# Three gaps of padding between the tiles of a gated cross-attention and expert kernel

## The chip, the cores and the metric

The kernel runs on one core of a Trainium2 chip. The time is that of one execution on the device, in microseconds. The median of three runs before the change is 463.22 us (463.19 to 463.77).

## What is computed

The input x is 16 batches of 128 tokens of 128 numbers. First comes a gated cross-attention: x is normalised, queries come from it, keys and values from a context of 77 rows of 96 numbers for each batch, with 16 heads of 8 numbers; the result goes through an output projection and is added to x with a gate. Then comes a gated mixture of experts over all 2048 tokens, in four rounds:

```
for r in range(4):
    logits = flat @ Wg[r] + bg[r]                 # four experts
    w = softmax(top 2 of logits)
    hmid = gelu(flat @ W1[e] + b1[e])             # 128 -> 512, every expert
    y = hmid @ W2[e] + b2[e]                      # 512 -> 128
    cur = cur + sum over e of w[e] * y[e]
```

All four experts are computed for every token, and each is weighed by its share, which is zero for two of them.

## The kernel before

All of it stands in SBUF, 128 partitions, in float32. The attention part runs batch by batch and ends at about 88 us; the transposes of the probabilities (L1275) use a stretch of the tile `below` as weights and the tile `ident` as moving operand, the sums over the values (L1297) use `v_st`, the sums of the probabilities (L1303) use `row_head`. The expert part is a loop over 64 units: four rounds, in each four chunks of 512 tokens, for each chunk four experts. Its order on every engine is written out by hand, and semaphores join the engines.

For precision each product is made of three matmuls. An operand is split in a high part, rounded to the format that TensorE takes (fp32r), and a low part, the remainder. A unit's first layer, `up(u)`, has four column blocks k; for each it issues high x high (L1395), low tokens x high weights (L1396) and high tokens x low weights (L1397), all 128x128 weights and 512 moving columns, into PSUM bank k. ACT takes the bank through the gelu into `g_sb` (L806) and makes `h_hi` (L813); DVE makes `h_lo` (L948). The second layer, `down(u)`, does the same three passes (L1408, L1409, L1410) over four blocks, all twelve into one PSUM bank, 4 or 5 by turns. DVE weighs the result (L958) and adds it to `cur` (L969). TensorE runs `up(u + 1)` before `down(u)`, so that the gelu of one unit stands beside matmuls of its neighbours. The last unit's second layer is done in two halves of 256 columns (L1423 to L1425).

Tiles are placed one after the other in the order in which the program declares them, each on a multiple of 32 bytes of a partition. In the program before, those of the two layers start at these bytes:

```
w1_hi  23648   w1_lo  31840      first-layer weights; block (e, k) is 2048 e + 512 k further
w2_hi  40032   w2_lo  48224      second-layer weights; the same steps
x_sb   56416   xn     65248   v_st 75104   probT 95584
cur   105824   x_lo  114016   x_hi 122208   tokens; chunk c is 2048 c further
cwb_even 132992   cwb_odd 149376   contrib 165760   g_sb 169856
h_hi  178048   h_lo  194432      activations; block k is 2048 k further, odd units 8192
```

`below`, `kT`, `q_st`, `k_st`, `xnT` and `ctxT` of the attention part share the bytes behind `cwb_even` with the tiles of the last two lines; `below` starts at 186272, and its second half (from block 5 on) is 2464 further in a partition.

Of the kernel before, what the change touches and what calls it, by code (L numbers as in the profile page):

```python
# [5 lines left out]
P = 128  # L6
# [9 lines left out]
def flamingo_gated_block(  # L16
# [59 lines left out]
    with ExitStack() as stack:  # L76
        def sb(name, shape, dt=F32):
            return stack.enter_context(nc.sbuf_tensor(name, shape, dt))
# [33 lines left out]
        lgs = sb("lgs", [P, 2, P])  # L112
        w1_hi = sb("w1_hi", [P, E * F], F32R)
        w1_lo = sb("w1_lo", [P, E * F], F32R)
        w2_hi = sb("w2_hi", [P, E * NF * D], F32R)
        w2_lo = sb("w2_lo", [P, E * NF * D], F32R)

# [12 lines left out]
        v_sb = sb("v_sb", [M, NC, NZ, HQ * DH, TC * PAIRS])  # L130
        probT = sb("probT", [P, 2, PAIRS * BLOCKS, L])

        cur = sb("cur", [P, N])
        x_lo = sb("x_lo", [P, NC, CH], F32R)
        x_hi = sb("x_hi", [P, NC, CH], F32R)
# [9 lines left out]
        wgt = sb("wgt", [P, TP, E])  # L145
        cw = sb("cw", [P, 2, E, TC])
        cwT = sb("cwT", [TP * E, P])
        cwb_even = sb("cwb_even", [P, 2, E, CH])

        attention = ExitStack()  # L150
# [1413 lines left out]
```

## Time and profile before

| | |
|---|---|
| median of the runs | 463.22 us |
| profiled execution, device time | 463.65 us |
| its span, first to last instruction | 461.9 us |
| TensorE busy | 452.0 us, 98% |
| DVE busy | 364.3 us, 79% |
| ACT busy | 359.9 us, 78% |
| GpSimd busy | 70.0 us, 15% |
| granted TensorE clock | 1.000 |

Matmuls are pipelined: one is counted as busy from its first read to its last result, while the next has already begun. Busy times of matmuls therefore add up to more than the time they take, and the pace is read from the distance between their starts.

### The profile page before, as it was taken

What the parts mean: (1) busy time and instruction counts of PE and PEld (TensorE: products, weight loads), DVE (VectorE), ACT (ScalarE), POOL (GpSimd) and SP (SyncE); (2) the same over time, 40 slices, a digit from 0 to 9 for tenths busy, and PEclk for the clock granted to TensorE, in tenths of its full rate; (3) what the DMA queues carried; (4) which work ended last, traced back from release to release, by engine and by line L of the source; (5) the groups of instructions that cost most, each with busy time, mean ns of one, the idle gap of its engine ahead of it and who ended that gap; (6) DMA issues with size and microseconds to landing.
All of it is one profiled execution on the core that took longest, in us unless ns stands there. A gap on an engine that the chain in (4) does not pass through costs nothing.

```text
span 461.9 us, 8784 instructions
## 1 busy us (share of the span) xinstructions
PE 452.0 (98%) x2856; PEld 355.4 (77%) x2856; DVE 364.3 (79%) x729; ACT 359.9 (78%) x742; POOL 70.0 (15%) x109
## 2 busy tenths in 40 slices
PE   8999999899999999999999999999999999999996
PEld 6666677678787888788878887888788878888885
DVE  6988989888878688768876887688768876887776
ACT  4777877696969779877987798778877887787873
POOL 6939884313000000000000000000000000000000
PEclk9999999999999999999999999999999999999999
DMA  6690000140020101300220022003100310023001
GB/s 163 191 202 17 1 9 11 32 154 3 0 92 24 70 2 43 143 0 1 67 118 1 1 87 99 0 2 113 72 0 0 141 45 1 0 80 128 24 0 45
DMA packets 12892, 25.18 MB, mean 55 GB/s; under 512 B 4615, under 2 KB 8496, under 8 KB 10800
## 3 DMA queue, kind: packets, MB, share of 16 engines
q1 hardware_dynamic: 9408, 22.23, 14.1%
q0 software_dynamic: 2784, 2.18, 2.6%
q8 instruction: 23, 0.38, 0.3%
q10 hardware_dynamic: 656, 0.23, 0.2%
q14 instruction: 21, 0.17, 0.1%
HBM read 22.82 MB, written 1.18 MB: 52 GB/s over the span
## 4 chain that ended last, share of the span: by engine, by line
PE 89%; DVE 6%; issue 2%; ACT 1%; DMA 1%; SPq 0%; POOL 0%; DVEq 0%; POOLq 0%
PE ps L1408 13%; PE ps L1410 13%; PE ps L1409 13%; PE ps L1395 12%; PE ps L1397 12%; PE ps L1396 12%; PE ps L1275 3%; PE ps L1297 2%; PE ps L1261 2%; PE ps L1303 2%; DVE least L897 1%; DVE rT_sb L913 1%; DMA x_sb<-in_x_dram 1%; PE ps L1310 1%; PE ps L1362 1%
## 5 line engine op out<-in xcount | busy, mean ns | idle before, releaser
L948 DVE TENSOR_TENSOR h_lo<-g_sb,h_hi 128x512 fp32r<-128x512 f32 x256 | 170.1, 688 | 76.0 <-ACT h_hi L813 76.0
L806 ACT ACTIVATE g_sb<-ps,cols 128x512 f32<-128x512 f32 x256 | 174.1, 691 | 41.4 <-PE ps L1397 40.8
L813 ACT ACTIVATE h_hi<-g_sb 128x512 fp32r<-128x512 f32 x256 | 155.5, 638 | 0.0
L1408 PE MATMUL ps<-h_hi,w_hi 128*128 128x512 f32 x252 | 102.4, 406 | 0.1
L1395 PE MATMUL ps<-x_hi,w_hi 128*128 128x512 f32 x256 | 101.0, 395 | 0.0
L1397 PE MATMUL ps<-x_hi,w_lo 128*128 128x512 f32 x256 | 100.1, 391 | 0.0
L1396 PE MATMUL ps<-x_lo,w_hi 128*128 128x512 f32 x256 | 99.8, 390 | 0.0
L1410 PE MATMUL ps<-h_hi,w_lo 128*128 128x512 f32 x252 | 99.6, 395 | 0.0
L1409 PE MATMUL ps<-h_lo,w_hi 128*128 128x512 f32 x252 | 99.4, 394 | 0.0
L1408 PEld LDWEIGHTS ps<-h_hi,w_hi 128*128 128x128 f32 x252 | 47.3, 188 | 14.0 <-issue 2.7
L1397 PEld LDWEIGHTS ps<-x_hi,w_lo 128*128 128x128 f32 x256 | 48.0, 188 | 11.4
L1396 PEld LDWEIGHTS ps<-x_lo,w_hi 128*128 128x128 f32 x256 | 48.1, 188 | 10.8
L1395 PEld LDWEIGHTS ps<-x_hi,w_hi 128*128 128x128 f32 x256 | 48.0, 188 | 10.8
L1410 PEld LDWEIGHTS ps<-h_hi,w_lo 128*128 128x128 f32 x252 | 47.2, 187 | 11.7
L1409 PEld LDWEIGHTS ps<-h_lo,w_hi 128*128 128x128 f32 x252 | 47.3, 188 | 9.9
L969 DVE TENSOR_TENSOR cur<-cur,contrib 128x512 f32<-128x512 f32 x63 | 43.2, 685 | 0.0
L723 ACT ACTIVATE probT<-ps 128x512 f32<-128x512 f32 (+1 forms) x48 | 25.0, 553 | 11.7 <-PE ps L1275 11.3
L713 ACT ACTIVATE below<-ps,least 128x77 f32<-128x77 f32 x128 | 29.3, 343 | 5.4 <-DVE least L897 5.3
L897 DVE TENSOR_REDUCE least<-ps 128x8 f32<-128x616 f32 x32 | 25.0, 790 | 0.4 <-PE ps L1261 0.4
L958 DVE SCALAR_TENSOR_TENSOR contrib<-ps,cols,cwb_even 128x512 f32<-128x512 f32 x32 | 23.9, 747 | 0.9 <-PE ps L1410 0.6
L1275 PE MATMUL ps<-ident,below 128*128 128x128 f32 (+1 forms) x160 | 24.0, 280 | 0.6 <-ACT probT L723 0.5
L739 ACT ACTIVATE th<-half_d 128x32 f32<-128x32 f32 (+1 forms) x10 | 2.3, 225 | 27.6 <-DVE half_d L1026 27.6
(126 smaller groups left out, 394.9 us busy)
## 6 DMA issues: line engine op xcount, KB each, us to landing
cwb_even<-cw_rows SPq DMA_DIRECT2D x8, 1024.0 KB, 5.5
cwb_odd<-cw_rows SPq DMA_DIRECT2D x8, 1024.0 KB, 4.9
w_hi<-in_L_ffn_W_dram POOLq DMA_DIRECT2D x2, 1024.0 KB, 10.4
w_in<-in_L_ffn_W_dram SPq DMA_DIRECT2D x1, 1024.0 KB, 5.6
x_sb<-in_x_dram SPq DMA_DIRECT2D x3, 256.0 KB, 5.1
out_dram<-xn SPq DMA_DIRECT2D x3, 256.0 KB, 2.5
ctxT<-in_ctx_dram SPq DMA_DIRECT2D x3, 115.5 KB, 4.7
v_st<-v_sb SPq DMA_DIRECT2D x14, 19.2 KB
```

Source lines behind the costliest of these rows:

```text
L806: nc.scalar.activation(g_sb[:, k, :], ps[:, k, :], ACT.Gelu_apprx_tanh, bias=b1_c[:, e * NF + k:e * NF + k + 1]).then_inc(gelu_done, 1)
L813: nc.scalar.activation(h_hi[:, u % 2, k, :], g_sb[:, k, :], ACT.Copy).then_inc(hi_done, 1)
L897: nc.vector.tensor_reduce(least[:, b % 2, :].rearrange("p (q h) -> p q h", q=NQ)[:, two, :], scores, AX.X, ALU.min).then_inc(least_done[ha ...
L948: nc.vector.tensor_tensor(h_lo[:, u % 2, k, :], g_sb[:, k, :], h_hi[:, u % 2, k, :].bitcast(F32), ALU.subtract).then_inc(lo_done, 1)
L969: nc.vector.tensor_tensor(cc, cc, contrib[:, u % 2, :], ALU.add).then_inc(added, 1)
L1275: t = tr(bank(key)[0:n, o:o + L], below[:, b % 2, at:at + n], ident[:, :])
L1395: mm(ps[:, k, :], w1_hi[:, w], x_hi[:, c, :], start=True, stop=False)
L1396: mm(ps[:, k, :], w1_hi[:, w], x_lo[:, c, :], start=False, stop=False)
L1397: mm(ps[:, k, :], w1_lo[:, w], x_hi[:, c, :], start=False, stop=True).then_inc(w1_done, 1)
L1408: mm(yb, w2_hi[:, w], hh, start=k == 0, stop=False)
L1409: mm(yb, w2_hi[:, w], hl, start=False, stop=False)
L1410: m = mm(yb, w2_lo[:, w], hh, start=False, stop=k == NF - 1)
```

## The change

Three tiles are declared that nothing reads or writes. The first, 32 bytes a partition, stands between the weights of the first and of the second layer. The second, 480 bytes, stands ahead of `cur`. The third, 768 bytes, stands ahead of `cwb_even`. Everything behind each is pushed along: the second-layer weights and the attention tiles behind them by 32 bytes, the tokens and the router's tiles by 512, `cwb_even` and all that follows by 1280. Instructions, their order and their semaphores stay.

```
         w1_lo = sb("w1_lo", [P, E * F], F32R)
+        pad_second = sb("pad_second", [P, 8])
         w2_hi = sb("w2_hi", [P, E * NF * D], F32R)
...
         probT = sb("probT", [P, 2, PAIRS * BLOCKS, L])
 
+        pad_tokens = sb("pad_tokens", [P, 120])
         cur = sb("cur", [P, N])
...
         cwT = sb("cwT", [TP * E, P])
+        pad_routes = sb("pad_routes", [P, 192])
         cwb_even = sb("cwb_even", [P, 2, E, CH])
```

## Rows read from the trace of the kernel before

**Rows 1.** Busy time of the engines, share of the span, instructions.
```profile
PE 452.0 (98%) x2856; PEld 355.4 (77%) x2856; DVE 364.3 (79%) x729; ACT 359.9 (78%) x742; POOL 70.0 (15%) x109
```

**Rows 2.** The chain that ended last, by engine and by line.
```profile
PE 89%; DVE 6%; issue 2%; ACT 1%; DMA 1%; SPq 0%; POOL 0%; DVEq 0%; POOLq 0%
PE ps L1408 13%; PE ps L1410 13%; PE ps L1409 13%; PE ps L1395 12%; PE ps L1397 12%; PE ps L1396 12%; PE ps L1275 3%; PE ps L1297 2%; PE ps L1261 2%; PE ps L1303 2%; DVE least L897 1%; DVE rT_sb L913 1%; DMA x_sb<-in_x_dram 1%; PE ps L1310 1%; PE ps L1362 1%
```

**Rows 3.** Windows of eight units: length, busy per engine, PEclk, DMA, GB/s.
```profile
220.00:264.00 44.00, 44.00 (x198) 35.03 (x197) 33.60 (x62) 35.27 (x65) 0.00 (x0) 1.00 0.13 49
```

**Rows 4.** Groups: shapes, count, busy us, mean ns, idle before, releaser.
```profile
L806 ACT ACTIVATE g_sb<-ps,cols 128x512 f32<-128x512 f32 x256 | 174.1, 691 | 41.4 <-PE ps L1397 40.8 <-DVE h_lo L948 0.4
L948 DVE TENSOR_TENSOR h_lo<-g_sb,h_hi 128x512 fp32r<-128x512 f32 x256 | 170.1, 688 | 76.0 <-ACT h_hi L813 76.0
L813 ACT ACTIVATE h_hi<-g_sb 128x512 fp32r<-128x512 f32 x256 | 155.5, 638 | 0.0
...
L1397 PE MATMUL ps<-x_hi,w_lo 128*128 128x512 f32 x256 | 100.1, 391 | 0.0
...
L1409 PE MATMUL ps<-h_lo,w_hi 128*128 128x512 f32 x252 | 99.4, 394 | 0.0
L1396 PEld LDWEIGHTS ps<-x_lo,w_hi 128*128 128x128 f32 x256 | 48.1, 188 | 10.8
...
L1409 PEld LDWEIGHTS ps<-h_lo,w_hi 128*128 128x128 f32 x252 | 47.3, 188 | 9.9
```

**Rows 5.** Timeline of one unit: start us, duration us, engine and line.
```profile
249.68 0.39 PE L1395 MATMUL ps<-x_hi,w_hi 128*128 128x512 f32 x1
...
251.07 0.39 PE L1395 MATMUL ps<-x_hi,w_hi 128*128 128x512 f32 x1
...
252.43 0.40 PE L1408 MATMUL ps<-h_hi,w_hi 128*128 128x512 f32 x1
252.43 0.19 PEld L1409 LDWEIGHTS ps<-h_lo,w_hi 128*128 128x128 f32 x1
...
255.23 0.40 PE L1395 MATMUL ps<-x_hi,w_hi 128*128 128x512 f32 x1
```

**Rows 6.** Timeline, head of another second layer, all engines.
```profile
257.99 0.40 PE L1408 MATMUL ps<-h_hi,w_hi 128*128 128x512 f32 x1
...
258.22 0.39 PE L1409 MATMUL ps<-h_lo,w_hi 128*128 128x512 f32 x1
...
258.45 0.40 PE L1410 MATMUL ps<-h_hi,w_lo 128*128 128x512 f32 x1
...
258.51 0.23 ACT L739 ACTIVATE th<-half_d 128x32 f32<-128x32 f32 x1 [3.32 <-DVE half_d L1026]
```

**Rows 7.** Timeline of TensorE, the loop's first first layer.
```profile
88.62 0.40 PE L1396 MATMUL ps<-x_lo,w_hi 128*128 128x512 f32 x1
...
90.00 0.39 PE L1396 MATMUL ps<-x_lo,w_hi 128*128 128x512 f32 x1
...
90.91 0.39 PE L1397 MATMUL ps<-x_hi,w_lo 128*128 128x512 f32 x1
```

**Rows 8.** Timeline of TensorE, last unit, first and twelfth half matmul.
```profile
454.43 0.28 PE L1423 MATMUL ps<-h_hi,w_hi 128*128 128x256 f32 x1
...
455.72 0.28 PE L1425 MATMUL ps<-h_hi,w_lo 128*128 128x256 f32 x1
```

**Rows 9.** Timeline of TensorE, two groups of four transposes of one batch.
```profile
79.81 0.60 PE L1275 MATMUL ps<-ident,below 128*104 128x128 f32 x4
...
80.60 0.60 PE L1275 MATMUL ps<-ident,below 128*128 128x128 f32 x4
```

**Rows 10.** Groups of weight loads of 32 columns.
```profile
L1303 PEld LDWEIGHTS ps<-probT,row_head 128*32 128x32 f32 x320 | 10.9, 110 | 0.3 <-issue 0.3
L1297 PEld LDWEIGHTS ps<-probT,v_st 128*32 128x32 f32 x320 | 10.6, 142 | 6.2 <-issue 6.2
```

More of the change, by code:

```diff
@@ L114, in flamingo_gated_block @@
         w1_lo = sb("w1_lo", [P, E * F], F32R)
+        pad_second = sb("pad_second", [P, 8])
         w2_hi = sb("w2_hi", [P, E * NF * D], F32R)
@@ L131, in flamingo_gated_block @@
         probT = sb("probT", [P, 2, PAIRS * BLOCKS, L])
+        pad_tokens = sb("pad_tokens", [P, 120])
         cur = sb("cur", [P, N])
@@ L147, in flamingo_gated_block @@
         cwT = sb("cwT", [TP * E, P])
+        pad_routes = sb("pad_routes", [P, 192])
         cwb_even = sb("cwb_even", [P, 2, E, CH])
```

## The prediction

> **What bounds the kernel now.** I read the busy shares first, then the chain of waits, then the windows, then the timeline of TensorE. The reader is to see in this order: TensorE is busy in 98% of the span, DVE and ACT in 79 and 78% [rows 1]; the chain that ended last is 89% TensorE, and its six largest lines are the six matmuls of the experts, 13% or 12% each [rows 2]; from 220 us to 264 us, eight units of the expert loop, TensorE has no idle time at all while ACT is busy for 35.27 us of 44 and DVE for 33.60 [rows 3]. So nothing that TensorE waits for matters in the expert loop; what counts is how fast one 128x512 matmul follows another. DVE and ACT wait for the others of the loop (76.0 us and 41.4 us of idle time before their two lines [rows 4]) and have room.
>
> Busy times of pipelined matmuls overlap (about 395 ns each [rows 4]), so the price of one is the distance from start to start. In one unit of the steady loop [rows 5] the second layer starts at 252.43 and the next first layer at 255.23: 12 matmuls in 2.80 us, 233.3 ns each. The first layer before it runs from 249.68 to 252.43: 12 in 2.75 us, 229.2 ns each, of which the first six take 1.39 us (231.7 each) and the last six 1.36 us (226.7 each). 512 columns at 2.4 GHz, the level that the granted clock of 1.00 in [rows 3] is, are 213.3 ns. So each matmul pays 13.4 ns over its columns at best and 20 ns in the second layer. The two layers have the same shapes, the same three passes, the same weight load (188 ns each in both [rows 4]) beside each matmul: the load of the next weights starts in the same hundredth as the matmul before it (252.43 and 252.43 in [rows 5]). What differs is which bytes are read, and which PSUM banks are written.
>
> I looked at three other explanations. Traffic of DVE and ACT: from 257.99 to 258.45, at the head of a second layer, ACT is at the end of 3.32 us of idle time and DVE does instructions of 32 columns, and the matmuls still come at 0.23 and 0.23 us, no faster than with both busy [rows 6]. Waiting: none. The break between layers: after a pause in which TensorE started no matmul of the experts, the first layer also has some slow ones, from 88.62 to 90.00 six in 1.38 us, then four in 0.91 us [rows 7]; so the slow start of the first layer is partly its own and is not all owed to the second layer. In the last unit, with 256 columns each, eleven second-layer matmuls take 1.29 us [rows 8], 117.3 ns against 106.7 ns for the columns: 10.6 ns over, about half of what the full ones pay. The surcharge grows with the length of the moving stream, as reads that disturb one another would.
>
> **The change part by part.** No instruction is added, removed or moved, no wait and no DMA changes; 1280 bytes a partition are left empty. What changes is where operands start.
>
> Second layer. w2_hi and w2_lo move from 40032 and 48224 to 40064 and 48256; h_hi and h_lo from 178048 and 194432 to 179328 and 195712. Modulo 64 bytes the weights stood at 32 and the moving operand at 0; afterwards both stand at 0. Their distance h_hi - w2_hi was 138016, which is 800 modulo 2048, and becomes 139264, which is 0 modulo 2048 (17 times 8192). In the first layer, the faster one, w1_hi at 23648 and x_hi at 122208 already agree modulo 64 (both 32) and modulo 256 (both 96); their distance is 98560, 256 modulo 2048. My reading is that the layer in which weight and moving operand disagree modulo 64 pays 6.6 ns more per matmul, and that the change takes this away. The trace does not prove it: it has one placement for each layer. If the second layer falls to the 226.7 ns of [rows 5], a unit saves 2.80 - 2.72 = 0.08 us. There are 63 full units (252 executions of each of the three lines [rows 4], four a unit), so 63 x 0.08 = 5.0 us. The bound on this side is that the first six of each first layer go to 226.7 too, 1.39 - 1.36 = 0.03 us a unit, 1.9 us more, 6.9 in all; [rows 7] speaks against it, so I leave it out of the sum. A further bound is the surcharge of the half matmuls, 10.6 ns: both layers at 223.9 ns would save 5.55 - 24 x 0.2239 = 0.18 us a unit, 11 us.
>
> First layer. w1 stays, x_lo and x_hi move by 512 to 114528 and 122720. Modulo 512 nothing changes (both at 352), modulo 1024 the distance goes from 256 to 768. The four weight blocks of a layer lie 512 bytes apart and so already run through both distances modulo 1024, and the last two blocks are equally fast in [rows 5]. I take nothing. The bounds: 1.9 us of gain (above), and on the other side the 233.3 ns of the other layer for all twelve, 12 x 0.2333 - 2.75 = 0.05 us a unit, 3.1 us of loss.
>
> What ACT, DVE and the stores read and write. cur by 512, cwb, contrib, g_sb by 1280, all by whole multiples of 256. Their instructions have steady durations (691, 638, 688 ns [rows 4]) and stand beside a full TensorE; they cost nothing as long as that covers them. If TensorE's unit shrinks to 5.47 us, ACT, with 4 x (691 + 638) ns = 5.3 us of overlapping work and 4.4 us of real busy time a unit (35.27 / 8), still fits. So no new wait is late next; TensorE stays the bound.
>
> The attention part, up to 88 us. x_sb, xn, v_st and probT move by 32, and below, kT, q_st and k_st by 1280. Here weight loads limit: four transposes take 0.60 us whether their block of `below` starts at 32 modulo 64 (all four of the group at 80.60) or at 0 (three of the four at 79.81) [rows 9]. So 32 bytes alone move nothing that is seen there. A weight load does feel how its columns lie: 32 columns of v_st, taken 32 bytes apart, take 142 ns where 32 adjacent ones of row_head take 110 [rows 10]; the step between them is not changed. I take 0, with 0.3 us to either side.
>
> Here the Trainium skill speaks against the change. Its page "TensorE: Matmul & The Clock Gate", section "Step-by-step: what each phase is for", says that TensorE has two independent SBUF read ports, one for the moving operand and one for the weights, so that loading does not take bandwidth from the running matmul. By that rule, neither layer should mind its placement and the time stays; that is the first rival below. The two layers' 229.2 and 233.3 ns don't follow from it, though they don't refute it. The page "SBUF — State Buffer", section "Specifications (TRN2)", gives cachelines of 16 bytes; all three shifts are multiples of 16, so by it too nothing would change, and no run here shows the size of such a line.
>
> Sum: the profiled execution took 463.65 us, span 461.9. 463.65 - 5.0 = 458.65. Against the median of 463.22 the same difference gives 458.2 us.
>
> **The rivals.** No change: the slower pace of the second layer belongs to something else, such as its twelve accumulations into one PSUM bank where the first layer changes banks every three. For it: the second and third passes of the first layer also stay in their bank; that speaks against. For it also: 32 bytes moved nothing in [rows 9]. Time 463.2.
>
> Slower: weight and moving operand of the second layer now start at the same byte modulo 8192, at the same moment [rows 5]. If the memory is built in parts by address, the two reads meet in one part from the first column, and the pace gets worse instead of better. That decides if disturbance comes from being in the same place, not from being out of step. Priced with another step of the size seen between the layers, 6.6 ns: 63 x 12 x 6.6 ns = 5.0 us, 468.2. The same rival in the other layer, if x at its new distance loses the 226.7 ns: 466.3. Both: 471.3.
>
> Smaller gain: only part of the second layer follows, as only half of the first does now: 2.5 us, 460.7. Larger gain: 6.9 us, 456.3, up to 452 by the bound of 11 us. With the back-to-back figure of 215.7 ns that the page "TensorE: Matmul & The Clock Gate" states, section "Wait — 56ns, not 53.3ns?", an estimate would be 24 x 63 x (231.3 - 215.7) ns = 24 us less; nothing in the trace comes near that pace beside weight loads.
>
> **How the numbers follow.** The forecast with the larger gain (452 to 459.5) has 0.46, the smaller gain 0.11, no change 0.17, slower 0.26 (second layer 0.15, first layer 0.08, both 0.03). What a measurement of this kernel can tell from no change is 0.2%, 0.9 us. So faster 0.57, same 0.17, slower 0.26. The likeliest case's own range is 455.5 to 459.5. The range for 8 in 10 reaches down to 454, which leaves out some 0.03, and up to 467.5, which takes in the loss in the first layer and leaves out most of the loss in the second, 0.16.
>
> **What would show it.** In the timeline of the changed kernel, the distance from the first L1408 to the next L1395 is 2.72 us if right, 2.80 for no change, 2.88 for the slower rival; the first layer stays at 2.75. TensorE stays without idle time from 220 to 440 us, the start of the expert loop stays at 88.3 us within 0.3, and the durations of L806, L813 and L948 stay within 5 ns (the idle time before them shrinks). The prediction is wrong in its cause if the gain sits in the first layer or before 88 us, or if DVE or ACT change their durations.

## The result, and the profile after

The changed kernel takes 460.79 us (median of 4 runs, 460.51 to 460.91) where the kernel before took 463.21 us beside it; the ratio is 0.9942, with a 95% interval from 0.9929 to 0.9954. That is 2.4 us faster. The forecast was 458.2 us, 5.0 us faster, with 455.5 to 459.5 as the range of its likeliest case and 454 to 467.5 as the range for 8 in 10.

The span of the profiled execution went from 461.9 to 459.1 us. The page of the kernel after shows where to look and where not: DVE is as busy as before [rows 1], TensorE 3.5 us less.

```profile
PE 448.5 (98%) x2856; PEld 355.1 (77%) x2856; DVE 364.3 (79%) x729; ACT 360.1 (78%) x742; POOL 70.1 (15%) x109
```

The window of the steady loop, for [rows 3], has TensorE without idle time as before, at the same clock, and two more matmuls in the same 44 us (200 for 198).

```profile
220.00:264.00 44.00, 44.00 (x200) 35.33 (x199) 33.96 (x64) 35.65 (x66) 0.00 (x0) 1.00 0.12 49
```

The groups of the kernel after, for [rows 4] (three lines further down in the program, so L951 is the old L948): durations on DVE and ACT are the same within 3 ns, the idle time ahead of them is 2.4 and 2.8 us less.

```profile
L951 DVE TENSOR_TENSOR h_lo<-g_sb,h_hi 128x512 fp32r<-128x512 f32 x256 | 170.1, 688 | 73.6 <-ACT h_hi L816 73.6
L809 ACT ACTIVATE g_sb<-ps,cols 128x512 f32<-128x512 f32 x256 | 174.7, 694 | 38.6 <-PE ps L1400 37.9
L816 ACT ACTIVATE h_hi<-g_sb 128x512 fp32r<-128x512 f32 x256 | 156.0, 641 | 0.0
```

The timeline of TensorE in the kernel after, for [rows 5] (start us, duration us):

```profile
251.26 0.39 PE L1411 MATMUL ps<-h_hi,w_hi 128*128 128x512 f32 x1
...
252.64 0.39 PE L1411 MATMUL ps<-h_hi,w_hi 128*128 128x512 f32 x1
...
254.01 0.39 PE L1398 MATMUL ps<-x_hi,w_hi 128*128 128x512 f32 x1
...
255.40 0.39 PE L1398 MATMUL ps<-x_hi,w_hi 128*128 128x512 f32 x1
...
256.76 0.39 PE L1411 MATMUL ps<-h_hi,w_hi 128*128 128x512 f32 x1
```

The second layer runs from 251.26 to 254.01: 12 matmuls in 2.75 us where it was 2.80. But it has taken on the form of the first layer: six matmuls in 1.38 us (230 ns each), then six in 1.37. The first layer from 254.01 to 256.76 is unchanged in length, 2.75 us, with its slow half still ahead of its fast one. Within it something moved. On the mean of the 35 that have second layers directly on both sides, its first matmul fell from 236.6 to 230.0 ns, and its last rose from 226.6 to 235.0.

For the sums below I took all start-to-start distances of the trace. A layer of 12 that nothing interrupts (35 second layers, 53 first layers) took 2.803 and 2.755 us before and takes 2.754 and 2.751 after. Over all 63 second layers, with those where a transpose stands ahead, the mean fell by 42 ns, 2.7 us in all; the first layers give 0.1 us and the start of the loop, 88.31 to 88.20 us, another 0.1. That is the 2.8 us of the span, within the rounding.

### The profile page after: what moved, and what is told of

It is laid out like the page before. It is cut to its first block, busy times and chain, and to the rows that moved or that the text cites. A ratio compares the mean times of both kernels' runs of the same rounds, so it can differ in the third digit from the quotient of the medians.

```text
span 459.1 us, 8784 instructions
## 1 busy us (share of the span) xinstructions
PE 448.5 (98%) x2856; PEld 355.1 (77%) x2856; DVE 364.3 (79%) x729; ACT 360.1 (78%) x742; POOL 70.1 (15%) x109
## 4 chain that ended last, share of the span: by engine, by line
PE 87%; DVE 6%; issue 3%; ACT 2%; DMA 1%; SPq 0%; POOL 0%; ACTq 0%; DVEq 0%; POOLq 0%
PE ps L1411 13%; PE ps L1413 12%; PE ps L1412 12%; PE ps L1398 12%; PE ps L1399 12%; PE ps L1400 12%; PE ps L1278 3%; PE ps L1300 2%; PE ps L1264 2%; PE ps L1306 2%; ACT g_sb L809 1%; DVE least L900 1%; DVE rT_sb L916 1%; DMA x_sb<-in_x_dram 1%; PE ps L1313 1%
## 5 line engine op out<-in xcount | busy, mean ns | idle before, releaser
L951 DVE TENSOR_TENSOR h_lo<-g_sb,h_hi 128x512 fp32r<-128x512 f32 x256 | 170.1, 688 | 73.6 <-ACT h_hi L816 73.6
L1412 PE MATMUL ps<-h_lo,w_hi 128*128 128x512 f32 x252 | 98.1, 389 | 0.0
```

Of the source, the lines that this page charges most:

```text
L951: nc.vector.tensor_tensor(h_lo[:, u % 2, k, :], g_sb[:, k, :], h_hi[:, u % 2, k, :].bitcast(F32), ALU.subtract).then_inc(lo_done, 1)
L1412: mm(yb, w2_hi[:, w], hl, start=False, stop=False)
```

## The experiments

All of them change placement alone. Two numbers describe each of them: the distance, modulo 256 bytes, from the weights' first byte to that of the moving operand in each layer (x_hi - w1_hi and h_hi - w2_hi; the low parts lie a multiple of 256 bytes away and have the same, except in e8, where both distances are given, high part first), and where the moving operands themselves stand modulo 256. Paces are the means of layers that nothing interrupts.

| kernel | distance, layers 1 / 2 | x, h at (modulo 256) | 12 matmuls, layers 1 / 2, us | time, us |
|---|---|---|---|---|
| before | 0 / 32 | 96, 128 | 2.755 / 2.803 | 463.2 |
| the change | 0 / 0 | 96, 128 | 2.751 / 2.754 | 460.8 |
| e1 | 64 / 64 | 160, 192 | 2.761 / 2.748 | 461.3 |
| e2 | 0 / 32 | 96, 128 | 2.755 / 2.803 | 463.4 |
| e3 | 32 / 0 | 128, 128 | 2.793 / 2.728 | 462.4 |
| e4 | 0 / 0 | 128, 128 | 2.721 / 2.720 | 457.6 |
| e5 | 0 / 128 | 96, 224 | 2.736 / 2.792 | 461.8 |
| e6 | 128 / 128 | 0, 0 | 2.789 / 2.789 | 464.6 |
| e7 | 96 / 192 | 0, 128 | 2.807 / 2.793 | 466.3 |
| e8 | 240 and 112 / 120 and 248 | 128, 0 | 2.798 / 2.802 | 465.8 |
| e9 | 0 / 0 | 96, 96 | 2.722 / 2.720 | 457.4 |
| e10 | 240 / 248 | 128, 128 | 2.799 / 2.768 | 464.1 |
| e11 | 224 / 160 | 128, 128 | 2.801 / 2.811 | 466.3 |

**e1, the 32 bytes without the large shifts.** The small gap ahead of the second-layer weights as in the change, and one of 32 bytes ahead of the tokens.

```
+        pad_second = sb("pad_second", [P, 8])
+        pad_tokens = sb("pad_tokens", [P, 8])
```

> Only the disagreement modulo 64 is mended: second-layer weights +32 bytes, tokens and activations +64 (x stays at 32 modulo 64 like w1, h stays at 0 modulo 64, now like w2). The distance h_hi - w2_hi is 832 modulo 2048, not 0. Theory 'phase' (weight and moving operand agree modulo 64): second layer 2.75 us per 12 matmuls instead of 2.80, time 460.4 to 461.2, the whole of the change's gain. Rival 'distance' (the gain is from the distance being 0 modulo 2048): second layer stays at 2.80 us, time 463.2.

461.28 us, ratio 0.9958 (0.9943 to 0.9973). Most of the gain is there (2.1 us of the 2.4), so 0 modulo 2048 is not what counts. But the plain rule of agreement modulo 64 isn't confirmed either: with 64 between the operands no layer settles at 226.7 ns; from the fourth on its matmuls run at 227.3 to 230.4, 228.8 on the mean, in both layers.

**e2, the large shifts without the 32 bytes.**

```
+        pad_tokens = sb("pad_tokens", [P, 128])
+        pad_routes = sb("pad_routes", [P, 192])
```

> The change without its 32 bytes: weights of both layers stay, tokens +512, activations +1280. Theory 'phase': the second layer still disagrees modulo 64, 2.80 us, first layer 2.75, time 463.0 to 463.5. Rival 'distance' (the large shifts bring it): the distance is 32 modulo 2048, nearly 0, second layer 2.75 to 2.77, time about 461.5.

463.36 us, ratio 1.0001 (0.9992 to 1.0011). The timeline shows the second layer from 251.98 to 254.78, 2.80 us, as before:

```profile
251.98 0.40 PE L1410 MATMUL ps<-h_hi,w_hi 128*128 128x512 f32 x1
254.78 0.40 PE L1397 MATMUL ps<-x_hi,w_hi 128*128 128x512 f32 x1
257.54 0.40 PE L1410 MATMUL ps<-h_hi,w_hi 128*128 128x512 f32 x1
```

The shifts of 512 and 1280 bytes do nothing by themselves; both are multiples of 256. The 32 bytes of the weights are the change.

**e3, the first layer put out of step.** The change, with the tokens 32 bytes further and the activations where the change has them.

```
+        pad_second = sb("pad_second", [P, 8])
-        pad_tokens = sb("pad_tokens", [P, 120])
+        pad_tokens = sb("pad_tokens", [P, 128])
-        pad_routes = sb("pad_routes", [P, 192])
+        pad_routes = sb("pad_routes", [P, 184])
```

> As the change, but the tokens are moved by 544 instead of 512 bytes, so x stands at 0 modulo 64 and w1 at 32; the second layer is that of the change. Theory 'phase': the first layer goes from 2.75 to 2.80 us per 12 matmuls, the second keeps 2.75 or less, so the time is back at about 463.5 to 464. Rival 'distance': 32 bytes more matter little, first layer 2.75, time 460.8.

462.41 us, ratio 0.9981 (0.9971 to 0.9990): slower than the change, but less than expected. The timeline:

```profile
249.16 0.39 PE L1398 MATMUL ps<-x_hi,w_hi 128*128 128x512 f32 x1
251.95 0.39 PE L1411 MATMUL ps<-h_hi,w_hi 128*128 128x512 f32 x1
254.68 0.39 PE L1398 MATMUL ps<-x_hi,w_hi 128*128 128x512 f32 x1
```

The first layer went from 2.75 to 2.79 us, as the theory of agreement asks: the slow pace has moved to the other layer with the 32 bytes, so it does not belong to the PSUM bank or to the layer. The second layer went to 2.73, better than in the change, though nothing of it was touched: its first matmul after the first layer already runs at 226.6 ns. What is new is that x and h stand at the same place modulo 256. And one matmul in it is slow: the last, beside which weights of the first layer are loaded, at a distance of 32 again (234.8 ns on the mean of 35 layers, its eleven neighbours 226.6 to 226.8). The first layer shows the same from the other side: its last matmul, beside which second-layer weights load at a distance of 0, takes 226.6 ns and the eleven before it 230.8 to 235.0. So it is the load beside a matmul whose distance counts.

**e4, all four operands at one place.** The gap of 32 bytes stands ahead of the first-layer weights instead of the second-layer weights.

```
+        pad_first = sb("pad_first", [P, 8])
+        pad_tokens = sb("pad_tokens", [P, 128])
+        pad_routes = sb("pad_routes", [P, 184])
```

> All four operands at 0 modulo 64: weights of both layers +32, tokens +544, activations +1280. Theory 'phase' in its plain form: both layers 2.75, time 460.8. Its stronger form (the six slow matmuls at each change of layer come from the two layers standing at different places modulo 64): both layers 12 x 226.7 ns = 2.72 us, 63 x 0.07 us less than the change, 456.5. Rival 'distance': first layer 2.75, second 2.75, 460.8.

457.64 us, ratio 0.9875 (0.9859 to 0.9892), 3.2 us better than the change. Where nothing interrupts them both layers take 2.72 us, with no slow start:

```profile
249.91 0.39 PE L1411 MATMUL ps<-h_hi,w_hi 128*128 128x512 f32 x1
252.63 0.39 PE L1398 MATMUL ps<-x_hi,w_hi 128*128 128x512 f32 x1
255.35 0.39 PE L1411 MATMUL ps<-h_hi,w_hi 128*128 128x512 f32 x1
258.07 0.39 PE L1398 MATMUL ps<-x_hi,w_hi 128*128 128x512 f32 x1
```

The time is 1.1 us above the 456.5 of the stronger form. The 28 second layers that follow a transpose or another matmul outside the experts still start slowly; e9, below, shows one.

**e5, all at 96 modulo 128.** Only the activations move, by 96 bytes; every gap named `pad_routes` stands ahead of `cwb_even`.

```
+        pad_routes = sb("pad_routes", [P, 24])
```

> Weights and tokens stay; only the activations move, by 96 bytes, so that all four operands stand at 96 modulo 128 instead of 0 as in the version with all at 0. If only the agreement counts: 226.7 ns for every matmul, 457.6 us. If the common place must be at the start of a 64- or 128-byte block: no better than the change, 460.8 us or more.

461.83 us, ratio 0.9967 (0.9952 to 0.9982). The time is in the range of the second outcome, but not for the reason written there: the second layer stayed slow, 2.792 us. At 96 modulo 128 it agrees with its weights, but modulo 256 it is 128 away, so this run doesn't tell whether the common place matters. It points to a period longer than 128, which e6 tests; e9 then puts all four at 96 modulo 256.

**e6, a distance of 128 in both layers.**

```
+        pad_first = sb("pad_first", [P, 8])
+        pad_tokens = sb("pad_tokens", [P, 160])
+        pad_routes = sb("pad_routes", [P, 184])
```

> As the version with all at 0, but tokens and activations 128 bytes further, so that moving operand and weights agree modulo 128 and disagree modulo 256. If the period is 128 bytes: 226.7 ns for every matmul, 457.6 us. If it is 256 bytes or more: slower, by the 233.3 ns of a disagreement up to 467.

464.60 us, ratio 1.0025 (1.0015 to 1.0034). It differs from e4 by 128 bytes between weights and moving operands and by nothing else, and both layers go from 2.72 to 2.79 us. The period is more than 128. In e4 the distance is 256 modulo 512 in the first layer and 0 in the second, and both are equally fast: the period that fits all runs here is 256 bytes.

**e7, distances of 96 and 192.**

```
+        pad_first = sb("pad_first", [P, 16])
+        pad_second = sb("pad_second", [P, 8])
+        pad_tokens = sb("pad_tokens", [P, 16])
+        pad_routes = sb("pad_routes", [P, 24])
```

> Both moving operands at 0 modulo 128, first-layer weights at 32 (distance 96 modulo 128), second-layer weights at 64 (distance 64). From the runs before: distance 64 gave about 228.8 ns, distance 32 gave 233.3, 0 gave 226.7. Expected: second layer 12 x 228.8 = 2.75 us; first layer, if a distance of 96 is like one of 32, 2.80 us; time about 463.5. If distance 96 behaved like 0 instead, the first layer would be 2.72 us and the time 459.

466.28 us, ratio 1.0058 (1.0043 to 1.0073), slower than expected by 2.8 us. What was called 64 modulo 128 here is 192 modulo 256, and it is not like the 64 of e1: 2.793 us where e1 had 2.748.

**e8, weights 16 and 8 bytes further.** The tiles of the weights are made 128 bytes longer and used from an offset; w1_lo is edited as w1_hi, and w2_hi and w2_lo with 2 in the place of 4.

```
+        pad_first = sb("pad_first", [P, 8])
-        w1_hi = sb("w1_hi", [P, E * F], F32R)
+        w1_hi = sb("w1_hi", [P, E * F + 32], F32R)[:, 4:4 + E * F]
...
+        pad_routes = sb("pad_routes", [P, 24])
```

> Moving operands at 0 modulo 128, first-layer weights 16 bytes further, second-layer weights 8 bytes further. If the block that counts is 32 bytes or larger and only its number matters: 226.7 ns in both layers, 457.6 us. If every byte of distance counts (the reads drift against one another): between 226.7 and 233.3 ns, the 16 bytes about 230 and the 8 bytes about 228, 460 to 461 us.

465.80 us, ratio 1.0050 (1.0035 to 1.0065). It decides nothing: the longer tiles put either the high or the low weights another 128 bytes off modulo 256, and a distance of 128 is slow by itself in e6. e10 repeats it without that.

**e9, one gap of 224 bytes.**

```
+        pad_routes = sb("pad_routes", [P, 56])
```

> One gap of 224 bytes and nothing else: activations move by 224, so that all four operands stand at 96 modulo 256. The runs so far fit a rule with 256 as its period: 226.7 ns where moving operand and weights agree modulo 256, 228.9 at a distance of 64, 232 to 234 at 32, 96, 128 and 192. By it: 226.7 ns for every matmul, no slow ones at a change of layer, 457.6 us, as good as the version with all at 0 modulo 64. If the common place must be a multiple of 64 or 128 bytes: 459.5 us or more.

457.35 us, ratio 0.9872 (0.9858 to 0.9887). The activations alone move, from 128 to 96 modulo 256, where the other three stand already. The timeline, with a start within each layer:

```profile
249.67 0.39 PE L1409 MATMUL ps<-h_hi,w_hi 128*128 128x512 f32 x1
...
251.03 0.39 PE L1409 MATMUL ps<-h_hi,w_hi 128*128 128x512 f32 x1
...
252.39 0.39 PE L1396 MATMUL ps<-x_hi,w_hi 128*128 128x512 f32 x1
...
253.75 0.39 PE L1396 MATMUL ps<-x_hi,w_hi 128*128 128x512 f32 x1
...
255.11 0.39 PE L1409 MATMUL ps<-h_hi,w_hi 128*128 128x512 f32 x1
```

Every half layer takes 1.36 us, 226.7 ns a matmul. The common place need not be a multiple of 64 or 128: 96 does as well as the 128 of e4. This is the version to keep: 224 bytes instead of 1280, and 3.4 us faster than the change. Its window of the steady loop holds 202 matmuls, and its distance to e4 (0.3 us) is within what the runs of either spread.

```profile
220.00:264.00 44.00, 44.00 (x202) 35.71 (x201) 34.41 (x64) 36.03 (x67) 0.00 (x0) 1.00 0.13 49
```

The slow start is not gone everywhere. Ahead of 28 of the 63 second layers stands a transpose or another matmul outside the experts, and all 28 start slowly here too, although x, h and all weights of the two layers stand at one place. Over their second to eighth matmul 24 of them lose 22 to 36 ns and three lose 10; the one left also waits. After the transpose at 221.28 the distances from the second matmul on are 231, 236, 228, 233 and 231 ns, then 226 to 227; e4 has the same.

```profile
221.28 0.27 PE L1384 MATMUL ps<-ident,cw 128*32 128x128 f32 x1
221.30 0.48 PE L1409 MATMUL ps<-h_hi,w_hi 128*128 128x512 f32 x1
221.62 0.39 PE L1410 MATMUL ps<-h_lo,w_hi 128*128 128x512 f32 x1
221.85 0.40 PE L1411 MATMUL ps<-h_hi,w_lo 128*128 128x512 f32 x1
222.09 0.39 PE L1409 MATMUL ps<-h_hi,w_hi 128*128 128x512 f32 x1
222.31 0.40 PE L1410 MATMUL ps<-h_lo,w_hi 128*128 128x512 f32 x1
222.55 0.39 PE L1411 MATMUL ps<-h_hi,w_lo 128*128 128x512 f32 x1
222.78 0.39 PE L1409 MATMUL ps<-h_hi,w_hi 128*128 128x512 f32 x1
223.00 0.39 PE L1410 MATMUL ps<-h_lo,w_hi 128*128 128x512 f32 x1
```

**e10, weights 16 and 8 bytes further, the rest in agreement.** The four tiles are edited as in e8, but 256 bytes longer, and the gap ahead of `cwb_even` is 224.

```
+        pad_first = sb("pad_first", [P, 8])
+        w1_hi = sb("w1_hi", [P, E * F + 64], F32R)[:, 4:4 + E * F]
...
+        pad_routes = sb("pad_routes", [P, 56])
```

> The run with weights 16 and 8 bytes further had, beside them, weights 128 bytes off modulo 256. This one has not: moving operands at 128 modulo 256, first-layer weights at 144, second-layer weights at 136. If the 32-byte block decides: 226.7 ns in both layers, 457.6 us. If every byte counts: both layers slower, between 226.7 and 233.3 ns, 459 to 463 us.

464.11 us, ratio 1.0015 (1.0005 to 1.0025). It is not a block of 32 bytes that decides: with 16 bytes between its operands the first layer is as slow as with 32 (233.2 ns a matmul), with 8 bytes the second takes 230.7 ns. The time is above the 463 that I gave as the end of that branch, as 16 bytes cost more than I took.

**e11, the two distances left.**

```
+        pad_first = sb("pad_first", [P, 16])
+        pad_second = sb("pad_second", [P, 16])
+        pad_tokens = sb("pad_tokens", [P, 40])
+        pad_routes = sb("pad_routes", [P, 56])
```

> The two distances modulo 256 not seen yet: 224 in the first layer (moving at 128, weights at 160), 160 in the second (weights at 224). By the rule that only agreement modulo 256 is fast: both 232 to 234 ns, 2.79 to 2.81 us per 12 matmuls, 466 us. If the sign matters (weights ahead of the moving operand by 32 instead of behind): first layer 2.75 us or less, 463.

466.34 us, ratio 1.0066 (1.0051 to 1.0081). Weights 32 bytes ahead are as slow as 32 behind. At 64 the sign does matter: 228.8 ns at a distance of 64 (e1), 232.7 at 192, which is 64 the other way (e7). Only 0 reaches 226.7.

```profile
250.49 0.40 PE L1399 MATMUL ps<-x_hi,w_hi 128*128 128x512 f32 x1
253.29 0.40 PE L1412 MATMUL ps<-h_hi,w_hi 128*128 128x512 f32 x1
256.10 0.40 PE L1399 MATMUL ps<-x_hi,w_hi 128*128 128x512 f32 x1
```

## Why the prediction was right, and where it was off

**What bounds the kernel: right.** TensorE has no idle time in the loop, and no duration on ACT or DVE changed. What was saved between two matmuls came through to the end: the layers gave 2.8 us, the span 2.8.

**The cause, weights and moving operand out of step in the second layer: right, with the wrong period.** e2 and e3 show it from both sides: without the 32 bytes there is no gain, and with 32 bytes between the operands of the first layer the slow pace is there. I had put the rule as agreement modulo 64. It is modulo 256 (e5, e6), and the change meets both, so the error did not show in its time. I had also written that 32 bytes alone move nothing for the transposes of [rows 9], and that is so there: from one transpose to the next of a group it is 118.0 ns on the mean before, 118.1 in e5 and 118.0 in e9, where `below` lies 96 and 224 bytes further from `ident`. With 128 moving columns it was no guide to the 512 columns of the expert loop. Nor was the other support, that the surcharge grows with the length of the moving stream [rows 8]: in agreement it is 13.3 ns for 256 columns (120 ns in e9) and 13.4 for 512, and out of step by 32 bytes the half matmuls were the faster ones. So of the arguments for the cause only the comparison of the two layers holds, and that had one placement for each: the guess was good, and in part lucky.

**The sum: the term of the second layer was mis-sized.** "A unit saves 2.80 - 2.72 = 0.08 us." It saved 0.042 on the mean, 2.7 us instead of 5.0. I priced the mended layer at the pace of the best half of the first layer, 226.7 ns, and not at its mean of 229.2. The row that would have said so was in hand: the first layer already agreed modulo 256 and still had six slow matmuls, so a layer mended in the same way was to be expected with them too: 63 x (2.80 - 2.75) = 3.2 us, 460.1. It is the case that I called the smaller gain, "only part of the second layer follows, as only half of the first does now", at 460.7 and with a chance of 0.11. Where nothing interrupts it, the mended layer takes 34 ns more than 12 x 226.7 ns; some 26 of them are its slow start and 8 its last matmul. The measured 460.8 lies outside the 455.5 to 459.5 of the likeliest case; that it lies in the range for 8 in 10 is owed to the width of that range, which reached up for the rivals.

**The slow start: "partly its own", half right.** I took it from [rows 7] that it would stay, and it did in the first layer, and came to the second. Between two layers that follow one another directly, e3, e4 and e9 show when it is gone: when x and h stand at the same place modulo 256, even where the first layer before it is slow throughout (e3). In the change the place goes from 96 to 128 and back, and the next five to seven matmuls are slow by 24 to 26 ns in all, although each agrees with its weights. With the last matmul of each layer, beside which the weights of the other layer load 32 bytes off (8 ns), that is what e9 removes, and it is worth 3.4 us, more than the change itself. Whether the new place brings the slow start or that one load out of step just before it, no run separates: where both layers agree with their weights, the one comes with the other. Nor is either needed: after a transpose it stands in e4 and e9 as well. At the start of the loop [rows 7], after a transpose with `ident`, e9 has it (231, 236, 228, 233 and 231 ns from the second distance on, as before) and e4, with x and w1 at 128, has not (226 to 227), so the pause alone is not its cause.

**The first layer and the attention part: nothing, right.** 2.755 to 2.751 us, and 88.31 to 88.20 us.

**The rivals.** The PSUM bank is refuted by e3 and e4. The collision of two reads that start at the same byte is refuted: a distance of 0 is the fastest of the ten modulo 256 that ran alone in a layer, and in the change itself the two start at the same byte modulo 8192 and the layer got faster. By the Trainium skill, "TensorE: Matmul & The Clock Gate", section "Step-by-step: what each phase is for", loading weights takes no bandwidth from the running matmul. The measured paces of 226.7 to 234 ns for the same instructions, told apart by placement alone, go against that as far as these 3% reach. What happens between the two reads inside, no run shows. The Trainium skill, "SBUF — State Buffer", section "Specifications (TRN2)", has cachelines of 16 bytes. In e10 the first-layer weights stand 16 bytes further from their moving operand, modulo 256, than in e4, and the pace goes from 226.7 to 233.2 ns; so it does not follow that a shift by whole lines changes nothing.

**Open.** Even in full agreement a matmul takes 226.7 ns for 213.3 ns of columns. Which part of these 13.4 ns the change of weights costs, and why, wasn't tried.

## What to carry to other kernels

Where TensorE is the bound and each matmul of 512 columns has a weight load beside it, let the tiles of weights and of moving operands start at the same byte modulo 256 in a partition, and all moving operands that follow one another too, and measure it. Here every block within a tile is a multiple of 512 bytes further, so the start of the tile decides for all of them; one gap of 224 bytes was worth 6.1 us of 463.45. Read the pace from start to start in the timeline and compare loops of the same shape inside one kernel: two layers at 229 and 233 ns with equal instructions were the sign of placement here. When a part is to be made like another, price it with the whole of that other part, slow start included. The rule is for 512 columns: for 256 the order of the distances was another.

## What the runs showed of the hardware that was not expected

- The same 8784 instructions take 457.35 to 466.34 us, 2.0% apart, by where the tiles lie alone.
- Pace of a 128x512 fp32r matmul with a weight load beside it, by distance modulo 256: 226.7 ns at 0; 228.8 at 64; 230.7 at 248; 232.4 at 128; 232.7 at 192; 232.8 to 233.6 at 32, 224 and 240; 233.9 at 96; 234.3 at 160.
- After the moving operand's place modulo 256 has changed from 96 to 128 or back, the next five to seven matmuls lose 24 to 26 ns in all, though every one agrees with its weights. A slow start also follows the 28 interruptions ahead of second layers by other matmuls, even with all four operands at one place (e4 and e9).
- Transposes of 128 columns do not feel it: 117.9 to 118.1 ns from one to the next of a group in all 13 kernels.
- For 256 columns the order is another: in the last unit the half matmuls take 120 ns at a distance of 0 and 117.8 at 32; at 64 the first half ran at 113.3 ns and the second at 117.6. There are only 24 of them here, and it wasn't followed up.
